# Summing squares in two steps: VectorE adds halves, TensorE sums four blocks in place of eight

## The chip, the cores and the metric

The kernel runs on one core of one Trainium2 chip. The metric is the device time of the whole program in microseconds, taken as the median of several runs. Of 3 runs of the kernel before the median is 2624.32 us (2620.51 to 2631.4).

Engines are called PE (TensorE's matrix multiply; PEld is its weight load), DVE (VectorE), ACT (ScalarE), POOL (GpSimd) and SP (SyncE, which here only starts transfers).

## The reference, cut to what matters

The program is a model of two layers on an input of 16 sequences by 512 tokens by 128 features: a Mamba-like state space block, a matrix product with signed weights, a gated linear attention (GLA) block and a mixture of 8 experts of which each token takes 2, each followed by a layer norm with a residual. The change touches the end of the attention block:

```
out = _gla_scan(q, k_gated, v, log_decay)          # b, s, 16 heads of 64
out = out.reshape(b, s, HID)                       # HID = 1024
out = out * rsqrt(mean(out * out, -1) + eps) * norm_w
out = out * sigmoid(x @ Wog.T)
return out @ Wo.T
```

The mean of squares runs over all 1024 features of one token. The kernel scales after the last product instead of before it: `norm_w` and constants are folded into `Wo`, so that for each token only the sum of the 1024 squares is needed beside the 128 outputs.

## The kernel before, in words

**Phases.** A first phase goes through the 16 sequences in rounds, software pipelined: in one round the state space block of sequence i, the attention of sequence j = i - 1 and the projections of sequence n = i + 1 are worked on side by side. A loop of 13 equal rounds stands between rounds that are written out (without one or two of the three). Then the expert phase multiplies 136 tiles of rows, and a last part mixes and stores.

**A round.** For the attention each engine runs first eight *units* (u = 0 to 7: the projections of q, gate and k for one pair of heads each, and, folded in, the *closing* of the sequence before: its last output product, residual, layer norm, routing), and then eight *stages* h = 0 to 7. A stage is one chunk of 128 tokens (c = h // 2) and one half of the heads (f = h % 2: 4 pairs, 8 heads). The order on each engine is written out by hand in functions `stage` and `body`; semaphores tie them.

**One stage on the engines.** PE fills for the next stage a value projection (L826), masks (L789 to L792) and scores (L804, L805), and for this stage the outputs (L856, L861) into `o_banks[:, f]`, an array of 128 features of a pair by 4 pairs times 128 tokens. The scores' bank is free for PE when DVE has added a chunk's update to the state (L1546, or L1548 in the first chunk). ACT squares the outputs into `sq[:, f, :]`, 128 by 512 (L1128, counted by `s_osq`). DVE, in its stage h, starts with `gate_out(h - 1)` (L1510: gate times outputs into `oT`, counted by `s_og`), then adds the state update (L1546 and L1548, two instructions of 64 partitions), then steps of the state space block of sequence i (scans L1405, products L1413 and L1398) between `decay_keys` (L1530) and `mask_scores` (L1503) of the next stage, then whatever layer norm and residual parts (L1520) fall in this stage. In stages 1 and 2 DVE also finishes the convolution of sequence n (L1440). POOL multiplies the decayed queries (L1906, `qd`), sums states by transfers (L1808), sends rows (L1886) and computes the root of the mean square (L1819, L1822).

**The output product.** `project_out(c)` on PE (L877) runs once per chunk, 64 times in all. For chunks 0, 1 and 2 it stands in stages 2, 4 and 6, late in the stage and ahead of that stage's outputs; for chunk 3 it stands in unit 0 of the next round. It waits for `s_og`, then multiplies 8 blocks of `oT` with `w_o` (L882), and 8 blocks of `sq` (as weights, 128 by 128) with one column of ones (L884), both into one bank. In float32 the profile lists two records for each such matmul: 16 for the eight. ACT copies the 129 columns out (`mixed`, L1133), POOL takes the root (L1819, L1822), DVE scales and adds the residual (L1520).

Of the kernel before, what the change touches and what calls it, by code (L numbers as in the profile page):

```python
# [7 lines left out]
P = 128  # L8
# [7 lines left out]
PAIRS = HEADS // 2  # L16
# [14 lines left out]
ALU = mybir.AluOpType  # L31
# [38 lines left out]
def at(it, per_round, k):  # L70

    return it * per_round + k


def after(eng, sem, value):

    if isinstance(value, int) and value <= 0:
        return
    eng.wait_ge(sem, value)
# [153 lines left out]
def build(nc, a, out):  # L233
# [6 lines left out]
    with ExitStack() as ctx:  # L240
# [3 lines left out]
        def sb(name, shape, dt=F32):  # L244
            return attention.enter_context(nc.sbuf_tensor(name, shape, dt))
# [39 lines left out]
        def sem(name):  # L285
            return ctx.enter_context(nc.semaphore(name))
# [31 lines left out]
        ones = sb("ones", [P, P])  # L318
# [46 lines left out]
        state = sb("state", [P, 2, PAIRS, 2 * DH])  # L365
        oT = sb("oT", [P, PAIRS, P])
        sq = sb("sq", [P, 2, T])
        mixed = sb("mixed", [P, 2, P + 1])
        rms = sb("rms", [P, TILES])
        attention.close()  # L370
# [94 lines left out]
        s_O = sem("o_filled")  # L465
        s_osq = sem("o_squared")
        s_og = sem("o_gated")
        s_half_state = sem("state_first_half")
        s_decst = sem("state_decayed")
        s_kept = sem("chunk_fall_kept")  # L470
# [66 lines left out]
        def drained(eng, ring, it, *uses):  # L537


            last = {}  # L540
            for use in uses:
                bank, count = ring.place[use]
                if bank not in last or count > ring.place[last[bank]][1]:
                    last[bank] = use
            for use in last.values():
                eng.wait_ge(ring.free_sem(use), ring.full_at(use, it))
# [3 lines left out]
        STAGES = 2 * TILES  # L550
# [130 lines left out]
        def _(pe):  # L681
            pe.wait_ge(s_weights, WEIGHTS)

            for t in range(TAPS):
# [3 lines left out]
                for c in range(HALVES):  # L688
                    mm = pe.matmul(ring_banks[:, 0, 0:2 * P], w_tap[:, c, :], pw[:, c, :],
                                   start=(c == 0), stop=(c == 1))  # L690
# [4 lines left out]
            def fill(ring, use, it, *needs):  # L695


                drained(pe, ring, it, *(n for n in needs if ring.place[n][0] != ring.place[use][0]))
                after(pe, ring.free_sem(use), ring.free_at(use, it))
                return ring.bank(use), ring.full_sem(use)  # L700
# [176 lines left out]
            def project_out(c, j, it):  # L877

                pe.wait_ge(s_og, at(j, STAGES, 2 * c + 2))
                bank, full = fill(ring, f"wo_{c}", it)  # L880
                for t in range(PAIRS):
                    pe.matmul(bank[:, 0:P], oT[:, t, :], w_o[:, t, :], start=(t == 0), stop=(t == PAIRS - 1))  # L882
                for t in range(PAIRS):
                    mm = pe.matmul(bank[:, P:P + 1], sq[:, t // 4, t % 4 * P:(t % 4 + 1) * P], ones[:, 0:1],  # L884
                                   start=(t == 0), stop=(t == PAIRS - 1))
                mm.then_inc(full, 1)

            def stage(h, i, j, n):
# [437 lines left out]
        def _(dve):  # L1326
# [179 lines left out]
            def gate_out(h, j):  # L1506
                c, f = divmod(h, 2)
                dve.wait_ge(s_osq, at(j, STAGES, h + 1))
                drained(dve, ring, j, *(f"og{m}_{c - c % 2}" for m in (2 * f, 2 * f + 1)))
                nc.vector.scalar_tensor_tensor(oT[:, 4 * f:4 * f + 4, :],  # L1510
                                               tog[:, 4 * f:4 * f + 4, c % 2 * P:(c % 2 + 1) * P], 1.0,
                                               o_banks[:, f, :].rearrange("p (t n) -> p t n", n=P), ALU.add, ALU.mult
                                               ).then_inc(s_og, 1)

            def residual(c, j):

# [533 lines left out]
```

## Time and profile before

| what | value |
|---|---|
| median of 3 runs | 2624.32 us (2620.51 to 2631.4) |
| the profiled execution: its own time | 2623.08 us |
| its span in the trace | 2621.2 us |
| mean granted TensorE clock | 0.936 of full speed |
| DVE instructions in the span | 3521 |
| L884, the matmuls with the column of ones | 1024 records, 123.4 us busy |
| L1510, `gate_out` on DVE | 128 instructions, 87.5 us busy |

The page gives the busy time of each engine and, in 40 equal slices, how busy it was. Busy time of PE is not PE at its peak, since matmuls overlap; what a group of matmuls takes is read from the start of its first to the start of what comes next. An entry such as "[0.17 <-DVE state L1548]" in a timeline says how long the engine stood idle ahead of this row, and what it waited for last. One line of a timeline may merge several instructions of a kind (x16).

### The profile page before, as it was taken

What the parts mean: (1) busy time and instruction counts of PE and PEld (TensorE: products, weight loads), DVE (VectorE), ACT (ScalarE), POOL (GpSimd) and SP (SyncE); (2) the same over time, 40 slices, a digit from 0 to 9 for tenths busy, and PEclk for the clock granted to TensorE, in tenths of its full rate; (3) what the DMA queues carried; (4) which work ended last, traced back from release to release, by engine and by line L of the source; (5) the groups of instructions that cost most, each with busy time, mean ns of one, the idle gap of its engine ahead of it and who ended that gap; (6) DMA issues with size and microseconds to landing.
All of it is one profiled execution on the core that took longest, in us unless ns stands there. A gap on an engine that the chain in (4) does not pass through costs nothing. (4 is left out here: it accounts for less than half of the span.)

```text
span 2621.2 us, 53454 instructions
## 1 busy us (share of the span) xinstructions
PE 2279.5 (87%) x17080; PEld 1685.0 (64%) x17081; DVE 1866.8 (71%) x3521; ACT 1354.7 (52%) x2568; POOL 818.0 (31%) x1092
## 2 busy tenths in 40 slices
PE   3499999999989898989898989898989939999990
PEld 1257565666667575757575757575757739999990
DVE  2795868686868677777777686858694437777777
ACT  2265656555655555565656555646564513333334
POOL 0111414141414141414232323322332333333336
PEclk9598999999999999999999989989999969999995
DMA  4431414141323232322222232313140022122216
GB/s 125 118 89 38 105 38 97 38 98 45 91 57 80 69 82 55 86 60 76 65 70 69 66 76 59 88 47 85 46 99 11 14 97 87 54 57 59 60 46 192
DMA packets 144249, 189.63 MB, mean 72 GB/s; under 512 B 17001, under 2 KB 92785, under 8 KB 143681
## 3 DMA queue, kind: packets, MB, share of 16 engines
q1 hardware_dynamic: 121808, 119.18, 15.5%
q0 software_dynamic: 22272, 67.92, 12.2%
q8 instruction: 141, 2.31, 0.4%
q14 instruction: 28, 0.22, 0.0%
HBM read 110.23 MB, written 27.56 MB: 53 GB/s over the span
## 5 line engine op out<-in xcount | busy, mean ns | idle before, releaser
L1405 DVE TENSOR_TENSOR_SCAN hs<-decay,push 128x512 f32<-128x512 f32 x256 | 354.4, 1406 | 23.8 <-ACT decay L1075 18.2
L984 PE MATMUL banks<-rowsT,w_here 128*128 128x128 f32 x2176 | 269.9, 278 | 5.9 <-DVE w_here L1729 5.8
L1503 DVE TENSOR_TENSOR S<-banks,S 128x512 f32<-128x512 f32 x256 | 164.2, 683 | 148.1 <-PE banks L804 143.5
L984 PEld LDWEIGHTS banks<-rowsT,w_here 128*128 128x128 f32 x2176 | 256.4, 194 | 9.3 <-issue 9.0
L1510 DVE SCALAR_TENSOR_TENSOR oT<-tog,banks 128x512 f32<-128x512 f32 x128 | 87.5, 684 | 238.2 <-ACT sq L1128 237.8
L1808 POOL DMA_DIRECT2D y<-ch x96 | 88.6, 923 | 512.0 <-DVE ch L1413 403.7
L1906 POOL TENSOR_TENSOR qd<-q,qd 128x512 f32<-128x512 f32 x96 | 134.5, 1401 | 302.5 <-ACT qd L1146 302.5
L1949 POOL DMA_INDIRECT results_scratch<-rows_out,result_to x136 | 131.9, 970 | 240.3 <-ACT rows_out L1283 233.3
L1108 ACT ACTIVATE S<-banks 128x512 f32<-128x512 f32 x272 | 162.4, 597 | 74.3 <-PE banks L792 48.0
L1272 ACT ACTIVATE tanh_h<-banks 128x512 f32<-128x512 f32 x136 | 81.3, 598 | 202.9 <-PE banks L984 168.9
L772 PE MATMUL banks<-x2T,w_k 128*128 128x512 f32 x256 | 138.1, 621 | 49.2 <-DVE k L1496 49.2
L1075 ACT ACTIVATE decay<-delta,a_neg 128x512 f32<-128x512 f32 x256 | 169.6, 711 | 17.7 <-DVE hs L1405 17.1
L1886 POOL DMA_INDIRECT rows_scratch<-x,row_now x128 | 162.1, 1266 | 40.1 <-issue 40.1
L1413 DVE TENSOR_TENSOR ch<-hs,c_all 128x1024 f32<-128x1024 f32 x128 | 155.9, 1218 | 3.5 <-DMA y<-ch 1.4
L1398 DVE TENSOR_TENSOR push<-du,b_all 128x1024 f32<-128x1024 f32 x128 | 155.8, 1217 | 0.1
L804 PE MATMUL banks<-q,k 64*128 64x128 f32 x1024 | 148.0, 285 | 8.8 <-DVE state L1546 5.8
L882 PEld LDWEIGHTS banks<-w_o,oT 128*128 128x128 f32 x1024 | 133.6, 208 | 29.9 <-issue 28.0
L1128 ACT ACTIVATE sq<-banks 128x512 f32<-128x512 f32 x128 | 76.2, 595 | 146.7 <-PE banks L861 146.5
L772 PE MATMUL banks<-x2T,w_q 128*128 128x512 f32 x256 | 151.9, 679 | 0.0
L805 PE MATMUL banks<-q,k 64*128 64x128 f32 x1024 | 148.0, 285 | 0.0
L715 PE MATMUL banks<-xT,w_conv 128*128 128x512 f32 x256 | 122.8, 625 | 27.6 <-ACT xT L1037 27.6
L1813 POOL TENSOR_TENSOR rstd<-var,minus_half 128x4 f32<-128x4 f32 x48 | 48.7, 1014 | 310.2 <-DVE var L1375 310.2
(222 smaller groups left out, 5540.5 us busy)
## 6 DMA issues: line engine op xcount, KB each, us to landing
y<-ch POOLq DMA_DIRECT2D x96, 512.0 KB
b_all<-bc_scratch SPq DMA_DIRECT2D x128, 256.0 KB, 5.3
c_all<-bc_scratch SPq DMA_DIRECT2D x128, 256.0 KB
rows_in<-rows_scratch SPq DMA_DIRECT2D x136, 66.0 KB
both<-results_scratch SPq DMA_DIRECT2D x32, 256.0 KB, 3.4
w<-w_dram SPq DMA_DIRECT2D x3, 2048.0 KB, 8.0
x_tok<-x_dram SPq DMA_DIRECT2D x16, 256.0 KB, 4.0
x_again<-x_dram SPq DMA_DIRECT2D x16, 256.0 KB, 3.0
```

The lines of the kernel that those rows point to most:

```text
L772: pe.matmul(bank, w[:, u * P:(u + 1) * P], x2T[:], start=True, stop=True).then_inc(full, 1)
L804: even = pe.matmul(low[:, at_h], k[0:DH, pair, here], q[0:DH, pair, here], start=True, stop=True)
L805: odd = pe.matmul(high[:, at_h], k[DH:P, pair, here], q[DH:P, pair, here], start=True, stop=True)
L984: mm = pe.matmul(bank_h[:, u % 2, n, here], w_here[:, u % 2, n, here], x, start=True, stop=True)
L1075: nc.scalar.activation(decay[:, n % 2, h, :], delta[:, h, :], ACT.Exp, scale=a_neg[:, h, n:n + 1]).then_inc(s_decay, 1)
L1108: nc.scalar.activation(dst, full(ring, use, j), func, scale=scale).then_inc(ring.free_sem(use), 1)
L1398: nc.vector.tensor_tensor(push[:], du[:], b_all[:, slot, :].unsqueeze(1).broadcast_to([P, HALVES, T]), ALU.mult).then_inc(s_push, 1)
L1405: nc.vector.tensor_tensor_scan(hs[:, h, :], decay[:, n % 2, h, :], push[:, h, :], 0.0, ALU.mult, ALU.add).then_inc(s_scan, 1)
L1413: nc.vector.tensor_tensor(ch[:, n % 2, :, :], hs[:], c_all[:, slot, :].unsqueeze(1).broadcast_to([P, HALVES, T]), ALU.mult).then_inc(s_ch, 1)
L1503: nc.vector.tensor_tensor(S[:, g, :], full(ring, f"S{g}_{c}", j), S[:, g, :], ALU.mult).then_inc(ring.free_sem(f"S{g}_{c}"), 1)
L1886: nc.gpsimd.indirect_dma_start(out=rows_dram, out_offset=bass.IndirectOffsetOnAxis(ap=row_now[:, n, t:t + 1], axis=0), in_=x3_rows[:, t, : ...
L1906: nc.gpsimd.tensor_tensor(qd[:, pairs, :], q[:, pairs, c * P:(c + 1) * P], qd[:, pairs, :], ALU.mult).then_inc(s_qd, 1)
```

## The change

After each `gate_out`, DVE adds the second half of `sq[:, f, :]` (pairs 2 and 3 of this half of the heads) to the first half (pairs 0 and 1), both 128 by 256, into a new tile `sq_less`, and counts it in a new semaphore. `project_out` waits for that count too, and sums 4 blocks of `sq_less` by the column of ones in place of 8 blocks of `sq`. Nothing else is changed.

```diff
+        sq_less = sb("sq_less", [P, 2, 2 * P])
...
+        s_sq_less = sem("squares_halved")
...
                 pe.wait_ge(s_og, at(j, STAGES, 2 * c + 2))
+                pe.wait_ge(s_sq_less, at(j, STAGES, 2 * c + 2))
                 bank, full = fill(ring, f"wo_{c}", it)
                 for t in range(PAIRS):
                     pe.matmul(bank[:, 0:P], oT[:, t, :], w_o[:, t, :], start=(t == 0), stop=(t == PAIRS - 1))
-                for t in range(PAIRS):
-                    mm = pe.matmul(bank[:, P:P + 1], sq[:, t // 4, t % 4 * P:(t % 4 + 1) * P], ones[:, 0:1],
-                                   start=(t == 0), stop=(t == PAIRS - 1))
+                for t in range(PAIRS // 2):
+                    mm = pe.matmul(bank[:, P:P + 1], sq_less[:, t // 2, t % 2 * P:(t % 2 + 1) * P], ones[:, 0:1],
+                                   start=(t == 0), stop=(t == PAIRS // 2 - 1))
                 mm.then_inc(full, 1)
...
                                                o_banks[:, f, :].rearrange("p (t n) -> p t n", n=P), ALU.add, ALU.mult
                                                ).then_inc(s_og, 1)
+                nc.vector.tensor_tensor(sq_less[:, f, :], sq[:, f, 0:2 * P], sq[:, f, 2 * P:4 * P], ALU.add
+                                        ).then_inc(s_sq_less, 1)
```

## Rows read from the trace of the kernel before

**Rows 1.** The page: busy time of all engines, and the slices of PE

```profile
PE 2279.5 (87%) x17080; PEld 1685.0 (64%) x17081; DVE 1866.8 (71%) x3521; ACT 1354.7 (52%) x2568; POOL 818.0 (31%) x1092
...
PE   3499999999989898989898989898989939999990
```

**Rows 2.** Stretches (length; busy PE, PEld, DVE, ACT, POOL; clock; DMA share, GB/s): loop, experts

```profile
255.30:1898.90 1643.60, 1513.36 (x11103) 1041.66 (x11103) 1217.37 (x2172) 955.06 (x1782) 512.79 (x676) 0.96 0.28 70
...
2125.00:2621.00 496.00, 391.09 (x3414) 386.77 (x3414) 364.33 (x838) 175.73 (x374) 209.19 (x279) 0.89 0.30 86
```

**Rows 3.** Timeline of PE: the sum of squares and what follows it

```profile
700.43 1.84 PE L884 MATMUL banks<-ones,sq 128*128 128x1 f32 x16
702.14 1.14 PE L856 MATMUL banks<-qd,state 128*128 128x128 f32 x8
```

**Rows 4.** Waits of PE, then of DVE, in one looped round, 757.7 to 884.0 us

```profile
PE banks L772 <- DVE k L1496: 2.8, 1, 2.8
PE banks L705 <- issue: 2.7, 1, 2.7
...
PE banks L804 <- DVE state L1548: 0.2, 1, 0.2
```

```profile
DVE oT L1510 <- ACT sq L1128: 15.8, 4, 7.4
DVE S L1503 <- PE banks L804: 8.6, 6, 2.3
```

**Rows 5.** Timeline of DVE over stages 1 to 3 of one round

```profile
690.09 1.22 DVE L1398 TENSOR_TENSOR push<-du,b_all 128x1024 f32<-128x1024 f32 x1
691.22 0.68 DVE L1440 SCALAR_TENSOR_TENSOR xc<-th,xc 128x512 f32<-128x512 f32 x1
691.82 0.68 DVE L1510 SCALAR_TENSOR_TENSOR oT<-tog,banks 128x512 f32<-128x512 f32 x1
692.42 0.86 DVE L1546 TENSOR_TENSOR state<-state,banks 64x256 f32<-64x256 f32 x2
...
704.98 0.69 DVE L1510 SCALAR_TENSOR_TENSOR oT<-tog,banks 128x512 f32<-128x512 f32 x1 [4.05 <-ACT sq L1128]
```

**Rows 6.** Timeline of PE, same round: the scores of stages 1 and 2

```profile
684.80 0.37 PE L804 MATMUL banks<-q,k 64*128 64x128 f32 x1 [0.17 <-DVE state L1548]
...
694.02 0.37 PE L804 MATMUL banks<-q,k 64*128 64x128 f32 x1
```

**Rows 7.** Timelines of POOL, DVE and PE: POOL's product beside DVE in two rounds

```profile
692.00 1.62 POOL L1906 TENSOR_TENSOR qd<-q,qd 128x512 f32<-128x512 f32 x1
```

```profile
1070.87 1.62 POOL L1906 TENSOR_TENSOR qd<-q,qd 128x512 f32<-128x512 f32 x1
...
1070.69 2.36 DVE L1440 SCALAR_TENSOR_TENSOR xc<-th,xc 128x512 f32<-128x512 f32 x1
...
1074.48 0.37 PE L804 MATMUL banks<-q,k 64*128 64x128 f32 x1 [0.93 <-DVE state L1546]
```

**Rows 8.** Timelines of DVE and ACT: waits around the start of a round

```profile
759.69 2.34 DVE L1405 TENSOR_TENSOR_SCAN hs<-decay,push 128x512 f32<-128x512 f32 x2 [1.29 <-ACT decay L1075]
...
767.92 0.35 DVE L1520 SCALAR_TENSOR_TENSOR x<-mixed,rms,x 128x128 f32<-128x128 f32 x1 [1.50 <-POOL rms L1822]
...
1130.43 0.60 ACT L1128 ACTIVATE sq<-banks 128x512 f32<-128x512 f32 x1 [0.26 <-PE banks L861]
```

**Rows 9.** Timeline of PE: the last output product of all

```profile
2115.67 2.05 PE L882 MATMUL banks<-w_o,oT 128*128 128x128 f32 x16 [1.42 <-DVE oT L1510]
```

**Rows 10.** PE ahead of and behind a wait; stretches of two rounds with different clocks

```profile
780.20 1.02 PE L772 MATMUL banks<-x2T,w_g 128*128 128x512 f32 x2
...
786.41 1.92 PE L772 MATMUL banks<-x2T,w_g 128*128 128x512 f32 x2
```

```profile
1387.50:1513.20 125.70, 114.93 (x854) 78.82 (x854) 92.42 (x168) 73.35 (x137) 40.11 (x52) 0.98 0.28 70
...
1642.50:1774.10 131.60, 122.21 (x854) 84.93 (x854) 94.25 (x168) 73.48 (x137) 39.32 (x52) 0.91 0.27 67
```

## The prediction, made before the changed kernel was run

> **What bounds the kernel now.** I read the page first. PE is busy for 87% of the span and shows eights and nines in nearly every slice, DVE for 71% [rows 1]. So PE looks like the limit, with DVE close behind; a share alone does not say what trading one for the other brings. The stretches put numbers on it: the 13 looped rounds take 1643.6 us, 126.4 each, of which DVE is busy for 93.6 [rows 2]. The expert phase of 496 us [rows 2] has none of the changed lines.
>
> Then PE's waits in one round [rows 4]. It stands still for a few microseconds only, above all 2.8 for DVE's keys (in the units), 2.7 for no recorded cause at the head of the loop, 0.2 for DVE's state update in stage 1. Outside these PE runs without a gap, so a microsecond taken from PE in a stage is a microsecond off the round, unless DVE, which works off its own queue, becomes late there. Where could it? In later stages it waits for ACT's squares ahead of `gate_out`, 4.05 us in stage 3 [rows 5] and 15.8 us over four times in a round, and 8.6 us over six times for PE's scores [rows 4]. In stages 1 and 2 it doesn't wait at all: `gate_out` follows the instruction before at 0.60 us [rows 5], and PE's scores wait 0.17 us for the state update behind it in stage 1 and none in stage 2 [rows 6]. This is the place where DVE's queue and PE's are level.
>
> **What is removed.** The 16 records of L884 take from 700.43 to 702.14, 1.71 us [rows 3]; half of them go, so 0.855 us per chunk, and 64 x 0.855 = 54.7 us for the program. The matmuls with one column are thus no cheaper than 0.107 us a record, and I take this row's spacing. The Trainium skill, page "TensorE: Matmul & The Clock Gate", section "Back-to-back issue gap", prices a matmul by its moving columns, about 60 cycles or 25 ns for up to 64 of them, which would make the eight records worth 0.2 us; the same section says that a stream of weight load and matmul pairs is set by both, and the measured row decides.
>
> **What is added on DVE.** No row shows a 128 by 256 add from SBUF. Rows on either side: 512 elements hold the queue for 0.60 us from start to start (691.22 to 691.82), 1024 for 1.13 (690.09 to 691.22) [rows 5]; 0.53 for 512 more elements gives 0.60 - 0.265 = 0.335 us for 256. The bounds are 0.60 above, the row with twice the elements, and 0.265 below, the slope alone. 128 adds are 43 us of DVE time. I take the row's slope. None can be a gain for DVE.
>
> **Which of these 43 us reach PE.** Take a looped round.
> - Stage 1 (add of half 0): the add is ahead of the state update for which PE's scores already wait 0.17 us [rows 6]. All of it counts, 0.34 us.
> - Stage 2 (add of half 1): behind `gate_out` at 691.82 the state update ends at 693.28, and the scores start at 694.02 [rows 5, 6], a slack of 0.74. With PE 0.34 later and DVE 0.67 later this would cover it. But POOL's product of `qd` runs from 692.00 to 693.62 [rows 7], and DVE's new add, which reads both inputs from SBUF, would start at about 692.76. How such a meeting ends is shown in another round: L1440, two SBUF inputs as well, takes 2.36 us in place of 0.68 and ends only after POOL's product, 1070.87 to 1072.49 [rows 5, 7]. So I let the add wait until about 693.7, end at 694.1, and the update of the state at 695.0 to 695.3; scores then start about 0.95 us later than before (bounds 0.34, no meeting, and 1.27 + 0.34 = 1.6, a whole product of POOL). In the three of 13 rounds where L1440 already met the product (PE waits 0.9 us there [rows 7], I count three such rounds) the first add disappears in that wait and only 0.34 us of the second is left. The mean is (10 x 0.95 + 3 x 0.34) / 13 = 0.81 us per round.
> - The same as a rule: the Trainium skill, page "SBUF — State Buffer", section "Who interferes with whom", says that a DVE instruction with two SBUF inputs and a GpSimd instruction that reads SBUF shut each other out for a whole instruction, whichever comes first; the trace agrees (2.36 us in place of 0.68), and were the two free of each other, the loss would be 0.34 per round in place of 0.81, 6 us less in all.
> - Stages 3 to 7: 24 us of waits for squares and scores lie around these adds [rows 4], 4.05 of them ahead of the add in stage 3 [rows 5]. I count nothing, even where POOL holds an add for a product. If this cover were gone in one stage, 0.34 us would be lost there, up to 1.6 with POOL. The tightest is stage 5, where update and scores stand close.
> - Around the head of the loop the adds of halves 6 and 7 delay DVE by 0.67 us, and ACT, which is busy with exponentials until 0.26 us ahead of the squares of half 6 [rows 8], can follow PE's gain of 0.855 only by 0.26. Together DVE falls back against PE by 0.59 + 0.67 = 1.26 us, and its wait for ACT's decay is 1.29 [rows 8]: just covered, with 1.50 us more at the wait for the root [rows 8].
> - In unit 0 the closing product's gain passes on, because DVE waits 1.50 us for the root [rows 8], and the whole chain of the units hangs on that.
> - PE's new wait in `project_out`: the sum of squares starts at 700.43 [rows 3], 7 us after the add of half 1 could be done, and the other chunks' products stand as late in their stages or, in unit 0, behind the whole head of a round. It costs something only in the last product of all, where PE already waits 1.42 us for `oT` [rows 9] and now for the add behind it, 0.42 us. Queued behind that wait are the sum, the root and the last layer norm, so there it counts.
>
> **The sum.** A looped round gains 4 x 0.855 - 0.81 = 2.61 us, 13 of them 33.9. The first attention round has three products: 2.6 - 0.34 = 2.2. The next to last has no convolution and its early stages wait for DVE: 3.4 - 4 x 0.34 = 2.1. The last: 3.4 - 0.42 = 3.0. Together 41.2 us. The profiled execution took 2623.1, so 2581.9; the median of the runs shown is 1.2 above it, and I say **2583 us**, 1.6% less.
>
> **Rivals.**
> 1. *DVE and POOL keep what PE gives.* If the adds of stages 1 and 2 both wait out a product of POOL and none is covered, a round loses 2 x 1.6 = 3.2 of its 3.4 us and the program gains some 10 us: 2614. Half of that gives 2600 to 2611. For it: DVE has no gap in these stages. Against: in stage 1 POOL sends rows (the code's order), and its product stands beside DVE's `gate_out` in stage 2.
> 2. *The sum of squares is cheaper than its row.* By a price per moving column 0.2 us per chunk would be gained and the 0.81 of a round still paid: 64 x 0.2 - 11 = 2 us, so about 2622. Against it stands the spacing of L884 [rows 3]. The page named above states that price.
> 3. *The clock, slower than before.* PE's granted clock is not full in all of a round: 0.98 in one of 125.7 us, 0.91 in one of 131.6 [rows 10]. It falls after PE's waits: a pair of 512 column matmuls takes 1.02 us ahead of the 2.8 us wait for the keys and 1.92 soon after it, half clock (1.2 in place of 2.4 GHz) [rows 10]. The change takes work from PE and adds to its waits in stages 1 and 2. If this left most rounds as the one of 131.6, a round would lose 5.2 us against the mean of 126.4 and gain 2.6: 13 x 2.6 = 34 us slower, less 7 in the other rounds, 2650. It decides from 2.6 us of lost clock per round on, half of what the worst row shows. Against: the added wait is about 1 us a round, beside 2.7 and 2.8 that are there already [rows 4].
> 4. That the change does not do what it says is ruled out by its text: two blocks of `sq_less` per half, two halves, four blocks, 128 adds.
>
> **How the numbers follow.** A measurement of this kernel can tell about 0.5% from no change, that is 13 us: faster means below 2611, slower above 2637. The forecast has 0.77, rival 1 half way 0.08 and in full 0.07, rival 2 0.03, rival 3 0.05. So faster 0.85, same 0.10, slower 0.05. The range: with nothing lost on DVE the gain is 54.7 us, 2569, and a few rounds with a clock like the better row of rows 10 give some 7 us more, 2562. Upwards a third of the rounds with the worse clock cost 22 us, 2605; that takes in half of rival 1. I give 2562 to 2606.
>
> **What the profile after should show.** L884 with 512 records and 0.85 us from its first to what follows; a group of 128 adds of 0.41 to 0.43 us each, some ten of them near 1.3 us, in stage 2; PE's wait for the state in stage 2 in most rounds, at 0.5 to 1 us, and 0.5 in stage 1; looped rounds of 123 to 124.5 us; the expert phase unchanged. I am wrong if the rounds stay at 126 us (then look whether DVE's state update or the clock took it), or if PE waits for the add in `project_out` in other places than the last.

## The result, and the profile after

Times are medians of device microseconds of whole runs; each ratio is to the kernel before on the same chip.

| | before | changed |
|---|---|---|
| median | 2622.64 us (2620.51 to 2631.4, 4 runs) | 2585.78 us (2581.34 to 2591.71, 4 runs) |
| ratio | | 0.9855, 95% interval 0.9824 to 0.9886 |
| profiled execution: span | 2621.2 us | 2578.3 us |
| from the end of the last sum of squares to the end of the span | 496.12 us | 496.09 us |

The change made the kernel 1.4% faster; 2583 us was forecast. What follows the last sum of squares takes as long as before, so the difference lies in the attention rounds.

Line numbers move: L772 (projections of the units) is L774 after, L804 is L806 (scores), L884 is L887 (sums of squares), L882 is L885, L1440 is L1443, L1503 is L1506, L1510 is L1513 (`gate_out`), L1546 and L1548 are L1551 and L1553 (state update), L1906 is L1911 (POOL's product). The new add is L1517.

The page after; the first line answers to [rows 1]. The groups below it are those of PE's sums, of the add and of the scores with their waits for the state; the last line is the scores' group in the kernel before.

```profile
PE 2210.4 (86%) x16568; PEld 1612.4 (63%) x16569; DVE 1924.6 (75%) x3649; ACT 1354.5 (53%) x2568; POOL 824.0 (32%) x1092
```

```profile
L887 PE MATMUL banks<-ones,sq_less 128*128 128x1 f32 x512 | 60.9, 240 | 0.0
L1517 DVE TENSOR_TENSOR sq_less<-sq 128x256 f32<-128x256 f32 x128 | 72.8, 569 | 0.0
L806 PE MATMUL banks<-q,k 64*128 64x128 f32 x1024 | 148.8, 286 | 20.9 <-DVE state L1551 12.3 <-DVE state L1553 8.0
...
L804 PE MATMUL banks<-q,k 64*128 64x128 f32 x1024 | 148.0, 285 | 8.8 <-DVE state L1546 5.8
```

PE is busy for 69.1 us less, DVE for 57.8 more. The idle time ahead of the scores, nearly all of it for the state, grew by 12.1 us over the program, from 8.8 to 20.9. The stretch of the 13 looped rounds, which answers to [rows 2] (same columns):

```profile
249.80:1864.00 1614.20, 1464.44 (x10686) 989.19 (x10686) 1265.94 (x2276) 955.08 (x1782) 515.96 (x676) 0.97 0.29 71
```

1643.6 became 1614.2, so 2.26 us a round. PE's timeline at the scores of stages 1 and 2, as in [rows 6], then at a sum of squares, as in [rows 3]. This is one of the five rounds in which POOL's product held L1443, hence the 1.28 (see stage 2 below):

```profile
677.57 0.37 PE L806 MATMUL banks<-q,k 64*128 64x128 f32 x1 [0.50 <-DVE state L1553]
...
688.13 0.37 PE L806 MATMUL banks<-q,k 64*128 64x128 f32 x1 [1.28 <-DVE state L1551]
...
694.54 0.95 PE L887 MATMUL banks<-ones,sq_less 128*128 128x1 f32 x8
```

The product of the next outputs starts at 695.36. The eight records hold PE from start to start for 0.82 us where sixteen held it for 1.71 [rows 3]: 0.89 saved per chunk. The wait in stage 1 is 0.50 where it was 0.17 [rows 6].

DVE's timeline in three places, with POOL's product beside the last two:

```profile
675.71 0.68 DVE L1513 SCALAR_TENSOR_TENSOR oT<-tog,banks 128x512 f32<-128x512 f32 x1
676.31 0.42 DVE L1517 TENSOR_TENSOR sq_less<-sq 128x256 f32<-128x256 f32 x1
676.64 0.87 DVE L1553 COPY state<-banks 64x256 f32<-64x256 f32 x2
...
559.56 0.69 DVE L1443 SCALAR_TENSOR_TENSOR xc<-th,xc 128x512 f32<-128x512 f32 x1
560.16 0.68 DVE L1513 SCALAR_TENSOR_TENSOR oT<-tog,banks 128x512 f32<-128x512 f32 x1
560.76 0.92 DVE L1517 TENSOR_TENSOR sq_less<-sq 128x256 f32<-128x256 f32 x1
...
709.51 1.37 DVE L1517 TENSOR_TENSOR sq_less<-sq 128x256 f32<-128x256 f32 x1
710.80 0.86 DVE L1551 TENSOR_TENSOR state<-state,banks 64x256 f32<-64x256 f32 x2
```

```profile
559.75 1.63 POOL L1911 TENSOR_TENSOR qd<-q,qd 128x512 f32<-128x512 f32 x1
...
709.33 1.27 POOL L1911 TENSOR_TENSOR qd<-q,qd 128x512 f32<-128x512 f32 x1 [7.24 <-ACT qd L1149]
```

With nothing beside it the add takes 0.42 us and holds the queue for 0.33 (676.31 to 676.64). Beside POOL's product it ends only behind it: at 561.68 in stage 2 (0.92 us, the product ends at 561.38), and in stage 4 at 710.88 (1.37 us, the product ends at 710.60). The add of stage 4 is as long as this in all 13 rounds; I had not counted it. PE's masks of that stage stand behind the turned keys (L814, L812 before) and wait for the same state update. They start 0.69 us behind these where they started 0.43 behind, after and then before:

```profile
711.03 0.60 PE L814 MATMUL banks<-eye,k 128*128 128x128 f32 x4
711.72 0.39 PE L791 MATMUL banks<-sel,fall_parts 112*128 112x512 bf16 x1
...
717.81 0.60 PE L812 MATMUL banks<-eye,k 128*128 128x128 f32 x4
718.24 0.38 PE L789 MATMUL banks<-sel,fall_parts 112*128 112x512 bf16 x1
```

**Where the time of a round went.** I read from PE's timeline the starts of eight landmarks in each looped round and took means over the 13; a round is counted here from its log decay product (L763, L765 after). "Chunk 0" is the stretch from the scores of stage 1 to the end of chunk 0's sum of squares, "chunk 1" from there to the end of chunk 1's, and so on; each of the four stretches marked * holds one sum of squares.

| stretch of PE | before | after | difference |
|---|---|---|---|
| head of the round to the end of the closing sum of squares * | 8.77 | 7.65 | -1.12 |
| units, to the value projection | 27.68 | 27.85 | +0.17 |
| value and gate projections to the scores of stage 0 | 11.00 | 11.88 | +0.88 |
| to the scores of stage 1 | 6.40 | 6.74 | +0.34 |
| chunk 0 (stage 2) * | 17.57 | 17.14 | -0.43 |
| chunk 1 (stages 3 and 4) * | 23.99 | 23.36 | -0.63 |
| chunk 2 (stages 5 and 6) * | 22.54 | 21.10 | -1.44 |
| to the end of the round | 8.48 | 8.46 | -0.02 |
| sum | 126.42 | 124.18 | -2.24 |

Four times 0.89 is 3.56. The adds take back 0.34 in stage 1 and 0.26 in stage 4 (0.89 - 0.63); stage 2 gives back 0.46 (0.89 - 0.43). The 0.17 more in the units comes from the first two rounds. What is left is the clock: chunk 2 and the head of the round ran at full clock (2.4 GHz) more often (0.55 and 0.23 gained beyond the 0.89), the value and gate projections more often at half (1.2 GHz), 0.88 lost:

```profile
532.71 2.05 PE L828 MATMUL banks<-w_v,x2T 128*128 128x512 f32 x2
534.55 3.62 PE L833 MATMUL banks<-x2T,w_og 128*128 128x256 f32 x8
...
908.80 1.10 PE L828 MATMUL banks<-w_v,x2T 128*128 128x512 f32 x2
909.74 1.89 PE L833 MATMUL banks<-x2T,w_og 128*128 128x256 f32 x8
```

The same matmuls take 2.05 and 3.62 us in one round and 1.10 and 1.89 in the other. The stretch is 10.77 us at full clock; it was longer in one of 13 rounds before and in seven after.

Outside the loop the changed kernel gained 5.3 us in the first attention round, 3.9 in the next to last and 4.2 from there to the last product. With 13 x 2.24 = 29.1 this is 42.5 of the 42.9 us between the spans.

### The profile page after: what moved, and what is told of

Read it like the earlier page. It is cut to its first block and busy times, and to the rows that moved or that the text cites. A ratio compares the mean times of both kernels' runs of the same rounds, so it can differ in the third digit from the quotient of the medians.

```text
span 2578.3 us, 52597 instructions
## 1 busy us (share of the span) xinstructions
PE 2210.4 (86%) x16568; PEld 1612.4 (63%) x16569; DVE 1924.6 (75%) x3649; ACT 1354.5 (53%) x2568; POOL 824.0 (32%) x1092
## 5 line engine op out<-in xcount | busy, mean ns | idle before, releaser
L1408 DVE TENSOR_TENSOR_SCAN hs<-decay,push 128x512 f32<-128x512 f32 x256 | 348.3, 1382 | 11.7 <-ACT decay L1078 5.9
L1506 DVE TENSOR_TENSOR S<-banks,S 128x512 f32<-128x512 f32 x256 | 164.1, 683 | 138.0 <-PE banks L806 138.0
L1513 DVE SCALAR_TENSOR_TENSOR oT<-tog,banks 128x512 f32<-128x512 f32 x128 | 87.6, 684 | 186.0 <-ACT sq L1131 185.8
L1911 POOL TENSOR_TENSOR qd<-q,qd 128x512 f32<-128x512 f32 x96 | 138.0, 1438 | 276.4 <-ACT qd L1149 276.4
L774 PE MATMUL banks<-x2T,w_k 128*128 128x512 f32 x256 | 139.1, 626 | 56.2 <-DVE k L1499 56.2
L1891 POOL DMA_INDIRECT rows_scratch<-x,row_now x128 | 167.5, 1309 | 40.1 <-issue 38.6
L806 PE MATMUL banks<-q,k 64*128 64x128 f32 x1024 | 148.8, 286 | 20.9 <-DVE state L1551 12.3
L774 PE MATMUL banks<-x2T,w_q 128*128 128x512 f32 x256 | 149.1, 667 | 0.0
L806 PEld LDWEIGHTS banks<-q,k 64*128 64x128 f32 x1024 | 124.2, 188 | 36.3 <-DVE state L1551 15.5
L828 PE MATMUL banks<-w_v,x2T 128*128 128x512 f32 x256 | 145.7, 652 | 0.0
```

The source lines that it names most:

```text
L774: pe.matmul(bank, w[:, u * P:(u + 1) * P], x2T[:], start=True, stop=True).then_inc(full, 1)
L806: even = pe.matmul(low[:, at_h], k[0:DH, pair, here], q[0:DH, pair, here], start=True, stop=True)
L828: pe.matmul(bank, x2T[:, here], w_v[:, f * T:(f + 1) * T], start=True, stop=True).then_inc(full, 1)
L1408: nc.vector.tensor_tensor_scan(hs[:, h, :], decay[:, n % 2, h, :], push[:, h, :], 0.0, ALU.mult, ALU.add).then_inc(s_scan, 1)
L1506: nc.vector.tensor_tensor(S[:, g, :], full(ring, f"S{g}_{c}", j), S[:, g, :], ALU.mult).then_inc(ring.free_sem(f"S{g}_{c}"), 1)
L1891: nc.gpsimd.indirect_dma_start(out=rows_dram, out_offset=bass.IndirectOffsetOnAxis(ap=row_now[:, n, t:t + 1], axis=0), in_=x3_rows[:, t, : ...
```

## The experiments

Twelve runs in four groups followed, two of them repeats of a kernel, each beside the kernel before on the same chip. The latter's median lay between 2619 and 2628 us from group to group, so times of different groups are compared to a few microseconds only; the changed kernel's 2585.78 belongs to a group of its own.

**1. What the adds cost: without them, and with nothing saved.**

```diff
-                pe.wait_ge(s_sq_less, at(j, STAGES, 2 * c + 2))
...
-                    mm = pe.matmul(bank[:, P:P + 1], sq_less[:, t // 2, t % 2 * P:(t % 2 + 1) * P], ones[:, 0:1],
+                    mm = pe.matmul(bank[:, P:P + 1], sq[:, t // 2, t % 2 * P:(t % 2 + 1) * P], ones[:, 0:1],
...
-                nc.vector.tensor_tensor(sq_less[:, f, :], sq[:, f, 0:2 * P], sq[:, f, 2 * P:4 * P], ALU.add
-                                        ).then_inc(s_sq_less, 1)
```

This is `four_no_add`, against the changed kernel; it leaves half of the squares out of the sum. `adds_eight_blocks` keeps the adds and the wait, and PE sums eight blocks of `sq` as in the kernel before.

> The add on DVE and the wait for it are taken out, and PE sums four blocks of sq, the first two pairs of each half of the heads: half of the squares are left out of the mean. This measures the gain on PE alone. Theory A (the four matmuls are worth 0.89 us per chunk as in the changed kernel's trace, and the adds cost PE's scores and masks 0.34 us in stage 1, up to 0.34 in stage 2 and 0.25 in stage 4): 2624 - 57 = 2567 us, about 15 below the changed kernel; scores of stage 1 wait 0.17 us for the state, as before the change. Theory B (the adds cost nothing, and what the change lacks to 57 us is a clock that fell in other places): within 4 us of the changed kernel, 2582 to 2590, with looped rounds of 124. Theory C (the matmuls are cheap, by columns): above 2600.

> DVE adds and PE waits for the add as in the changed kernel, but PE sums the eight blocks of sq as before the change. This measures the cost of the adds and of the wait alone. Theory A: slower than before the change by 0.34 + 0.25 + up to 0.34 us per round, some 10 to 15 us: 2634 to 2640. Theory B: the time of before within 4 us, 2620 to 2628. If the adds made more meetings with POOL's product than the changed kernel's trace shows, more than 2645.

Measured: 2572.19 us (4 runs, ratio 0.980, 0.9754 to 0.9846) without the adds; 2632.75 us (10 runs, ratio 1.0026, 0.9995 to 1.0058) with the adds and nothing saved. So the adds where they stand cost some 7 us set against the kernel before, an interval that takes in nothing at all and a value between the two theories' ranges, and 13.6 set against the changed kernel of another group, near theory A. PE's half is worth 45 (the ratios 1.0026 to 0.9855) to 54 us (the kernel before to `four_no_add`). The stretches of PE are sharper than the times. In the table's stretches `four_no_add` has 6.40 where the changed kernel has 6.74 and 23.10 where it has 23.36, in every round: 0.34 and 0.26 us belong to the adds of stages 1 and 4. In chunk 0 its full clock value is 16.44, 0.89 below the 17.33 of before, where the changed kernel has 16.60 in its best rounds. `adds_eight_blocks` has 6.74 in stage 1 too and 24.25 in chunk 1 where the kernel before has 23.99: the same 0.34 and 0.26, paid with nothing saved. The value and gate projections were at half clock in 8 of 13 rounds without the adds, and in 2 of 13 with the adds and eight blocks: that loss doesn't come from the adds.

**2. The add behind the state update.** Same work, other order on DVE: `gate_out`, state update, then the add.

```diff
-                nc.vector.tensor_tensor(sq_less[:, f, :], sq[:, f, 0:2 * P], sq[:, f, 2 * P:4 * P], ALU.add
-                                        ).then_inc(s_sq_less, 1)
...
+            def halve(h):
+                f = h % 2
+                nc.vector.tensor_tensor(sq_less[:, f, :], sq[:, f, 0:2 * P], sq[:, f, 2 * P:4 * P], ALU.add
+                                        ).then_inc(s_sq_less, 1)
...
                     add_update(h, j)
+                    if h:
+                        halve(h - 1)
```

> The add moves behind the state update of the same DVE stage; nothing else differs from the changed kernel. Theory A: scores of stage 1 wait 0.17 us again (6.40 us from the scores of stage 0 to those of stage 1, in place of 6.74), the held add of stage 4 no longer holds the masks (23.10 us from the end of chunk 0's product to that of chunk 1, in place of 23.36), together 0.6 to 0.9 us per round: 2572 to 2578 against 2586. Theory B: no change beyond what the clock scatters, 2580 to 2592.

Measured: 2572.22 us (6 runs, ratio 0.980, 0.9764 to 0.9836), theory A, and the same as `four_no_add` in the same group, as if the adds were not there. The group of PE's scores and DVE's timeline in stage 4, which is late enough for POOL's product (705.97 to 707.24) to have the state update beside it in place of the add:

```profile
L806 PE MATMUL banks<-q,k 64*128 64x128 f32 x1024 | 148.8, 286 | 14.0 <-DVE state L1554 11.0 <-DVE state L1556 3.0
```

```profile
705.56 0.68 DVE L1513 SCALAR_TENSOR_TENSOR oT<-tog,banks 128x512 f32<-128x512 f32 x1
706.16 0.86 DVE L1554 TENSOR_TENSOR state<-state,banks 64x256 f32<-64x256 f32 x2
707.05 0.47 DVE L1520 TENSOR_TENSOR sq_less<-sq 128x256 f32<-128x256 f32 x1
```

The state update, which has one input in PSUM, takes 0.86 us beside the product as elsewhere; the add behind it takes 0.47. The adds of stages 3 and 5 now meet a product, 0.94 us in most rounds, and PE doesn't wait for them. The stretches are 6.40, 16.44 at best and 23.10, those of `four_no_add`.

**3. Two blocks in place of four.** With the adds behind the state update, DVE sums further, either by one `tensor_reduce` from 512 to 128 columns or by a second add from 256 to 128; PE multiplies two blocks. The first two lines are the edit of `reduce_to_two`, the others that of `two_adds_behind_state`.

```diff
-                nc.vector.tensor_tensor(sq_less[:, f, :], sq[:, f, 0:2 * P], sq[:, f, 2 * P:4 * P], ALU.add
+                nc.vector.tensor_reduce(sq_less[:, f, 0:P], sq[:, f, :].rearrange("p (x n) -> p n x", n=P), AX.X, ALU.add
...
+                dve.wait_ge(s_sq_less, at(j, 2 * STAGES, 2 * h + 1))
+                nc.vector.tensor_tensor(sq_less[:, f, 0:P], sq_less[:, f, 0:P], sq_less[:, f, P:2 * P], ALU.add
```

> Behind the state update DVE sums all four pairs of a half in one tensor_reduce, 512 elements to 128, and PE sums two blocks per chunk. Two blocks fewer are worth 4 x 0.107 = 0.43 us per chunk, 27 us in all. The reduce should hold DVE for 0.60 us like other instructions of 512 elements, in place of 0.335, so 34 us more on DVE. Theory A (PE is the limit, DVE's time counts only where the state update stands in front of PE's scores): 27 us less than with the add behind the state, less 0.27 us in stage 2 of each round: 2546 to 2555. Rival (DVE is the limit in stages 0 to 3): its 0.27 more per half counts at four halves a round, 14 to 18 us, and the result is 2560 or above.

> Behind the state update DVE adds halves (256 elements) and then quarters (128), with a wait for the first add between them, and PE sums two blocks per chunk. Theory A (the reduce of 512 to 128 failed because it takes 1.05 us, and DVE's time counts where x2's layer norm and the state update stand behind it): two adds hold DVE for some 0.34 + 0.25 = 0.6 us, two blocks fewer are worth 0.43 us per chunk, so up to 27 us less than with one add behind the state (2572): 2548 to 2560; the close of a round's head then shows no wait for x2. Rival (the rounds are held by DVE and by the clock whatever PE saves): 2568 to 2576, like the reduce.

Measured: 2573.31 us (6 runs, ratio 0.9802, 0.9763 to 0.9842) with the reduction; 2593.82 us (6 runs, ratio 0.9884, 0.9856 to 0.9913) with the second add. The reduction takes 1.05 us, not the 0.68 I had assumed from other instructions that read 512 columns, and the time is that of four blocks, in the rival's range and not in theory A's 2546 to 2555:

```profile
L1519 DVE TENSOR_REDUCE sq_less<-sq 128x128 f32<-128x512 f32 x128 | 134.1, 1048 | 2.5
```

PE's chunks shrink (16.27, 22.65 and 20.28 us at best), but the units grow from 27.82 in `add_behind_state` to 28.31. That the longer DVE queue does this is likely and was not tried by itself.

The time with the second add lies outside both ranges, theory A's and the rival's. The add is short, 0.29 us, and PE's stretches shrink as they should (chunk 0 to 15.99, chunk 1 to 22.65 at full clock). But DVE now stands still at the head of 12 of the 13 looped rounds, with no cause in the profile's waits, and the units, which hang on it, grow from 27.85 in the changed kernel to 30.28 us in the mean. DVE's timeline there, its group of that line, and the queue that brings instructions:

```profile
877.31 0.42 DVE L1519 TENSOR_TENSOR sq_less<-sq 128x256 f32<-128x256 f32 x1
877.76 0.29 DVE L1522 TENSOR_TENSOR sq_less<-sq_less 128x128 f32<-128x128 f32 x1
880.82 1.23 DVE L1400 TENSOR_TENSOR push<-du,b_all 128x1024 f32<-128x1024 f32 x1 [2.77 <-issue]
```

```profile
L1400 DVE TENSOR_TENSOR push<-du,b_all 128x1024 f32<-128x1024 f32 x128 | 155.7, 1217 | 34.2 <-issue 34.1
```

```profile
q14 instruction: 89, 0.72, 0.1%
```

That queue has 28 packets in the kernel before. The kept traces give each packet's time. In the kernel before, q14 has none from 363 to 1914 us. All other kernels here have the same: five packets in the first looped round and none in the twelve behind it. `two_adds_behind_state` has five in each of the 13, and three of them stand at the pause: 876.8, 878.8 and 881.2 us, around DVE's idle time from 878.05 to 880.82. So it looks as if the instructions of DVE's longer loop were brought in anew in each round; that these packets are DVE's is read from where they stand. The pause of PE at the head of the loop, the 2.7 us without a recorded cause in [rows 4], has its like: the other instruction queue, q8 (140 to 142 packets in every kernel), has two or three at each of the twelve heads of the loop where PE pauses, so at 501.1 and 504.1 us in the kernel before, where PE starts at 503.7 after 3.06 us of idle time.

**4. What makes the clock fall at the value projection.** First the 2.8 us wait for the keys is filled: in unit 5 PE computes the gate matmul four times over, with the same result.

```diff
+                    for _ in range(3 if name == "g" and u == 5 else 0):
+                        pe.matmul(bank, w[:, u * P:(u + 1) * P], x2T[:], start=True, stop=True)
```

> The changed kernel, but in unit 5 PE computes the gate projection four times into its own bank (the same values each time) before it tells ACT, so that it multiplies for 2.6 us in place of waiting 2.8 us for DVE's keys. Theory D (what a looped round loses against PE's saving is half clock on the value and gate projections, 10.77 us from their start to the scores at full clock, 12.1 to 13.7 at half, and it follows the wait for the keys): the stretch is 10.77 in all or nearly all 13 rounds, and the mean round falls by 0.9 us and more: 2566 to 2576 against 2586. Rival (the half clock there has another cause, such as the wait at the head of the loop): 7 of 13 rounds long as before, 2582 to 2592.

> The same repetition in the kernel before the change, where the value and gate projections ran at half clock in one of 13 rounds only. Theory D: the half clock that followed the wait fell on the units, which DVE holds anyway, so little is gained: 2616 to 2628. If PE's repetition itself delays the gate for DVE, 2630 to 2640.

Measured: 2594.11 us (6 runs, ratio 0.9903, 0.9871 to 0.9935) for the changed kernel so filled, 2626.32 us (10 runs, ratio 1.000, 0.9976 to 1.0025) for the kernel before. The wait is gone, yet in the changed kernel the value and gate projections ran at half clock in 9 of 13 rounds, and the time is 2 us above the rival's range. This wait isn't the cause. The kernel before so filled is in theory D's range; its value and gate projections were at half clock in 1 of 13 rounds, but another half clock moved. It had stood in the units, behind the wait, in 9 of 13 rounds; now it was gone from there, and chunk 2 was long (23.2 us or more) in 11 rounds in place of 6.

Two short waits stand closer, 1.4 us for the last keys and 1.35 us for the table of chosen experts. Where PE's units behind the 2.8 us wait run at half clock, PE reaches the last keys later, and the first of the two waits isn't there. This is the last 12 us ahead of the value projection in one round of each kernel (columns as in [rows 2]; the clock is the third number from the end), the kernel before first:

```profile
655.60:667.60 12.00, 8.57 (x21) 3.88 (x22) 11.47 (x22) 5.59 (x11) 2.06 (x2) 0.86 0.65 150
...
520.70:532.70 12.00, 7.18 (x22) 3.30 (x23) 11.47 (x22) 5.48 (x11) 2.08 (x2) 0.96 0.66 152
```

```profile
529.99 1.13 PE L774 MATMUL banks<-x2T,w_k 128*128 128x512 f32 x2 [1.37 <-DVE k L1499]
```

In the kernel before, 9 of 13 rounds are like the first line, without a wait for the last keys, and the value projection was at full clock in all nine. The changed kernel has four such rounds, again all at full clock; its other nine have both short waits, and seven of them the half clock. In the looped rounds of all fourteen kept traces together the value projection was at half clock in none of the 66 without both waits and in 72 of the 116 with both. So much of what looks like a new loss is a half clock that moved: in the units DVE is busy for 11.47 of the 12 us and their length is the same at either clock, at the value projection it costs 1.4 to 3 us.

In the last group both short waits are filled.

```diff
+                    for _ in range(3 if name == "g" and u == 7 else 0):
+                        pe.matmul(bank, w[:, u * P:(u + 1) * P], x2T[:], start=True, stop=True)
...
+                    bank, full = fill(ring, "rank", it)
+                    for _ in range(3):
+                        pe.matmul(bank, w_g[:, u * P:(u + 1) * P], x2T[:], start=True, stop=True)
                     pe.wait_ge(s_chosen, at(j, HOT_STEPS, HOT_STEPS - 1))
-                    bank, full = fill(ring, "rank", it)
```

> The changed kernel with PE's two short waits right ahead of the value projection filled: in unit 7 the gate matmul is computed four times (1.4 us wait for the last keys) and three more matmuls of 512 columns stand ahead of the wait for the table of chosen experts (1.35 us). Results are the same. Filling the 2.8 us wait further ahead had changed nothing (half clock on value and gate projections in 9 of 13 looped rounds, 2594 us). Theory E, that these two waits set off the fall of the clock at that place: value and gate projections at full clock in at least 11 of 13 rounds and 2573 to 2578 us, up to 12 us below the changed kernel. Theory F, that the clock falls by what PE has done over a longer time and the place only moves: the half clock stays in 7 or more rounds there, or moves to the keys and masks behind it, 2585 to 2595 us.

Measured: 2634.25 us (12 runs, ratio 1.0027, 1.0011 to 1.0042). PE's timeline of the end of the units in one round:

```profile
925.65 2.79 PE L946 MATMUL banks<-x2T,w_g 128*128 128x512 f32 x6
928.28 0.18 PE L949 MATMUL banks<-hot_bf,earlier 128*128 128x32 bf16 x1
928.31 0.18 PE L950 MATMUL banks<-hot_bf,ones_bf 128*128 128x32 bf16 x1
928.34 1.10 PE L830 MATMUL banks<-w_v,x2T 128*128 128x512 f32 x2
```

The value and gate projections ran at full clock in 13 of 13 rounds, which is theory E's mark; in the changed kernel's two profiles they did so in 6 and in 3. But the time did not follow: it lies outside both theories' ranges, some 45 us above the changed kernel by the ratios. Part of it is my filling, which was twice too long: three matmuls hold PE for 2.6 us, not 1.3, and the units grew from 27.6 to 29.6 in a typical round. Another part is theory F's mark: chunk 2 now had the half clock value of 22.3 us or more in 10 of 13 rounds, where the changed kernel had it in 3, and took 22.17 us in the mean in place of 21.10. The round grew by 2.67 us in the mean, which makes 35 of the 56 us between the profiled spans; the other 21 lie outside the loop and were not traced. So with these two waits filled the clock no longer fell at that place and fell more often elsewhere. Whether the missing waits or the added matmuls did it, this run can't tell.

**5. Side by side on one chip.** The changed kernel again; the add late in stages 1 and 2 only; late in all stages; and, with the adds late in all stages, one second add per chunk for both halves together, so that DVE has three adds per chunk where `two_adds_behind_state` has four. The first diff is that of `late_in_stages_1_2`, the second that of `one_second_add_per_chunk`.

```diff
                     if h:
                         gate_out(h - 1, j)
+                    if h > 2:
+                        halve(h - 1)
                     add_update(h, j)
+                    if h in (1, 2):
+                        halve(h - 1)
```

```diff
+            def halve_again(c, j):
+                dve.wait_ge(s_sq_less, at(j, STAGES, 2 * c + 2))
+                nc.vector.tensor_tensor(sq_less[:, :, 0:P], sq_less[:, :, 0:P], sq_less[:, :, P:2 * P], ALU.add
+                                        ).then_inc(s_sq_two, 1)
...
                 state_part(m, 1, i)
+                if j is not None and h and h % 2 == 0:
+                    halve_again(h // 2 - 1, j)
```

> The changed kernel once more, as it stands, so that the others of this group can be set against it directly. Expected 2585.8 us as before, within 5 us.

> The changed kernel with the add behind the state update in stages 1 and 2 only; in stages 3 to 7 it stays ahead of it. It tells which stages made up the 13 us that moving all adds brought (2585.8 to about 2572). Theory A, my prediction's: only stages 1 and 2 have no cover, so this kernel has the whole gain, 2572 us. Theory B: the adds of stage 4, held by POOL's product to 1.37 us in all looped rounds, cost some 0.26 us per round, 3.4 us in all, and the tail of this adds up elsewhere; then this kernel stays at 2575 to 2577 us. Theory C: the gain came from stages 3 to 7 alone, 2583 to 2586 us.

> The same kernel as add_behind_state, beside the others of this group. Expected 2572 us, 13 to 14 us below the changed kernel (ratio to it 0.995); had the earlier difference come from the chip of that group, the two would be within 4 us.

> The adds of all stages behind the state update, and once per chunk one more add that takes both halves from 256 to 128 columns; PE then sums two blocks. DVE gets 3 instructions per chunk, between the 2 of the changed kernel and the 4 of the one with two adds for each half. PE saves another 0.41 us per chunk, 26 us in the program; DVE pays 0.34 us more per chunk, in even stages and at the head of the loop. Theory A, that DVE has the room and only the pause at the head of the loop took the gain of the kernel with four instructions: 2560 to 2565 us, without the 2.8 us pause. Theory B, that the pause comes with every longer loop: as with four instructions, 2585 to 2594 us. Theory C, that DVE's own time is the limit now: 2570 to 2575 us without the pause, with longer waits of PE for keys or state.

| kernel | median, runs | ratio to before, 95% interval |
|---|---|---|
| changed_again | 2586.73 us, 6 | 0.9876 (0.9853 to 0.9899) |
| late_in_stages_1_2 | 2584.60 us, 4 | 0.9871 (0.9854 to 0.9888) |
| late_in_all_stages | 2580.12 us, 5 | 0.9844 (0.9825 to 0.9863) |
| one_second_add_per_chunk | 2558.12 us, 5 | 0.9775 (0.9758 to 0.9791) |

Moving all adds brought 6.6 us here, half of what was expected and with intervals that overlap, and 13.6 across the groups before. What the traces show of it is 0.34 and 0.26 us in every round (stretches 6.74 to 6.40, 23.36 to 23.10), and in chunk 0 0.16 us in six rounds (16.60 to 16.44) and 0.65 in two, together 10 us in the loop, between the two. `late_in_stages_1_2` has 6.40, 16.44 and 23.36, so it keeps just stage 4's 0.26; this says which add costs what. Its time, 2.1 us below the changed kernel where 13 x 0.50 = 6.5 were due, doesn't separate the three theories: a round of one kernel varies by more than that with the clock. The changed kernel's own second profile has a span of 2592.5 us, 14.2 above the first, with 10 rounds of 13 at half clock in the value and gate projections.

`one_second_add_per_chunk` is the best of all kernels here, 28.6 us below the changed kernel on the same chip and 61.1 below the kernel before, with intervals that don't touch. It lies just below theory A's range. Its groups of the adds, of the line that had paused, and the instruction queue:

```profile
L1520 DVE TENSOR_TENSOR sq_less<-sq 128x256 f32<-128x256 f32 x128 | 69.7, 544 | 2.5
L1525 DVE TENSOR_TENSOR sq_less<-sq_less 128x256 f32<-128x256 f32 x64 | 42.0, 657 | 1.7
L1401 DVE TENSOR_TENSOR push<-du,b_all 128x1024 f32<-128x1024 f32 x128 | 155.7, 1217 | 2.0 <-issue 1.9
```

```profile
q14 instruction: 28, 0.23, 0.0%
```

DVE has no pause, and the queue is back at 28 packets. Each stretch with a sum of squares is 0.45 us shorter at full clock than with four blocks (15.99, 22.65 and 20.28 in place of 16.44, 23.10 and 20.73).

## Why the prediction was right, point by point

- **What bounds the kernel.** Right: time taken from PE in a stage came off the round, and the one price is DVE's state update. The stretches of `adds_eight_blocks` show the price alone, those of `four_no_add` the gain alone. One reading was too short: PE did not run "without a gap" outside the three waits named. The same view of waits lists four more in that round, 1.3 us for the table of chosen experts, 1.0 for the residual and twice 0.7, and two of these stand in the units.
- **What is removed.** 0.855 us per chunk by halving the row; 0.89 measured (0.82 left of 1.71). In the program 2.2 us more. Rival 2, by which eight such records would be worth 0.2 us, is out; a record with one column costs 0.82 / 8 = 0.103 us. The rule of the Trainium skill's page "TensorE: Matmul & The Clock Gate", section "Back-to-back issue gap", that prices a matmul by its moving columns doesn't give this number; the same section says that pairs of weight load and matmul are set by both, and with that the trace agrees: the weight loads of L887 start 0.11 us apart, as its matmuls do.
- **What is added.** 0.335 us of queue per add; 0.33 measured, and 0.42 us of duration. Right.
- **Stage 1.** 0.34 us predicted, 0.34 measured; the wait of 0.50 is as named.
- **Stage 2.** Together with stage 1, 0.81 was predicted and 0.34 + 0.46 = 0.80 came out, but not by the steps given. I let the add wait out POOL's product in ten rounds and end 1.3 us after its start. It was longer than usual in eight rounds, 0.91 to 0.94 us in six and 1.41 in two, since the product had started earlier beside it (559.75, the add at 560.76), and the scores came 0.16 us late in the six and 0.65 in the two. The other part: the product caught L1443, as in [rows 7], in five rounds in place of three, with 1.3 us of wait each in place of 0.9. It does so in six rounds of `add_behind_state` too, where no add stands ahead of the state update, so the add alone doesn't make it. That the sum fits is in part luck. Which of two meeting instructions has to wait can't be read from their recorded starts alone: the product is recorded 0.18 us behind L1440 at 1070.87 and held it [rows 7], and 0.19 us behind L1443 at 559.75 and did not (0.69 us).
- **Stages 3 to 7.** Counted at nothing, "even where POOL holds an add for a product". This step failed: the add of stage 4 was held to 1.37 us in all 13 rounds, and PE's masks of that stage, which wait for the same update, started 0.26 us late, 3.4 us in the loop. I had taken stage 5 for the tightest place and looked at scores only. The add is recorded 0.18 us behind the product's start and ends only behind its end (709.51 and 709.33, 710.88 and 710.60). That fits the Trainium skill, page "SBUF — State Buffer", section "Who interferes with whom", by which a DVE instruction with two SBUF inputs contends with a GpSimd instruction that reads SBUF and the order of issue decides who is blocked; the mistake was to give it no cost here. `four_no_add` and `add_behind_state`, which have 23.10 in chunk 1, and `late_in_stages_1_2`, which keeps 23.36, agree on it.
- **The clock.** Not in the sum, and within the rounds it came out near nothing: 0.88 lost at the value projection, 0.78 gained in chunk 2 and at the head of the round. Rival 3 didn't come, but the half clock moved, from the units to the value projection among other places (experiment 4). In `filled_end_of_units` it left one place and stood more often in another.
- **Outside the loop.** 7.3 us predicted in three parts (2.2, 2.1, 3.0), 13.4 found (5.3, 3.9, 4.2). In the first attention round and in the next to last one, one sum of squares each had run at half clock before, 3.27 us; in the changed kernel it takes 0.82, which is 2.45 in place of 0.89. More of the same clock stands around them: chunk 2 of the first attention round took 25.33 us and now 20.73, 3.7 more than the sum's 0.89. The mean round had hidden that these rounds have clocks of their own. The 1.2 us above the forecast behind the next to last round were not traced. The wait in the last product rose as forecast from 1.42 [rows 9] to 1.80 us, 1.84 expected, and PE waited for the add in `project_out` in no other place:

```profile
2073.65 2.02 PE L885 MATMUL banks<-w_o,oT 128*128 128x128 f32 x16 [1.80 <-DVE oT L1513]
```

- **The sum.** 2.61 us a looped round predicted, 2.24 found: +0.14 for the larger saving, -0.26 for stage 4, -0.10 for the clock, and -0.15 in the units and in rounding. In the loop 4.8 us too much, outside it 6.1 too little; so the forecast for the profiled execution, 2581.9, met 2581.34 by two errors of opposite sign.

What stays open: by what rule the clock falls, and why it falls in the units in 9 looped rounds of the kernel before and in 4 of the changed one, which leaves both short waits and the half clock at the value projection to the others. Rounds with both waits at full clock exist too (3 of 4 before, 2 of 9 after), so the waits alone don't decide it. At what length of DVE's loop the packets and the pause begin was not tried; one add per chunk lies between the two kernels.

## What to carry to other kernels

Work that another engine reads late belongs behind the instruction that another engine reads next: the same 128 adds cost 0.6 us and more of a round's 124 ahead of the state update (7 to 14 us in the medians) and nothing in these stretches behind it. When a sum over partitions is made by a column of ones with a new 128 by 128 block of weights each time, each record costs TensorE 0.10 us here, so it pays to fold blocks elsewhere first, and to fold with few wide instructions: with one second add over both halves the time fell by 28.6 us, with two narrow ones DVE's loop began to pause. Filling an engine's waits to hold its clock should be judged by the whole round: the stretch that it aims at can be cured while the time gets worse.

## What the runs showed that I had not expected

- A float32 `tensor_reduce` from 512 to 128 columns with its four inputs 128 columns apart took 1.05 us, where instructions of DVE with 512 contiguous columns take 0.68 (L1513 above). Whether the operation or the distance of its inputs makes the difference was not separated.
- With four adds per chunk in place of three DVE's loop pauses for 2.8 us at its head, and the instruction queue has 89 packets in place of 28, five in each looped round.
- The half clock of the value projection vanished in all 13 rounds when two waits of 1.4 and 1.35 us ahead of it were filled, and showed up some 60 us later, in chunk 2.
